# Cross-attention and routed FFN on one core: transposed activations stored by token tile in DRAM, and a store moved on ACT

## The reference

```python
a = einsum('bqd,bkd->bqk', layernorm(x), ctx)
x = x + einsum('bqk,bkd->bqd', softmax(a), ctx)
n = layernorm(x)
base = einsum('bsi,oi->bso', n, base_w) + base_b       # 2048 x 2048
h = einsum('bsi,ri->bsr', n, A)                        # rank 64
probs = softmax(einsum('bsi,ei->bse', n, router_w))    # 16 experts
topw, topi = top_k(probs, 2); topw /= sum(topw) + 1e-6
x = x + base + 0.5 * sum over the two experts of topw * (h @ B[expert].T)
```

## Time and profile before

| what | us |
|---|---|
| median of 3 runs | 1431.38 (1430.12 to 1438.4) |
| the profiled execution | 1436.82 |
| its span | 1433.4 |
| PE busy | 1361.7 (95%) |
| DVE busy | 935.2 (65%) |
| ACT busy | 623.8 (44%) |
| POOL busy | 320.4 (22%) |
| PE granted clock, mean | 0.989 |

### The profile page before, as it was taken

One profiled execution on the slowest core, in us unless ns is written; L12 is line 12 of the kernel. 1 busy time (PEld: TensorE's weight loads), 2 busy tenths in 40 slices (PEclk: granted clock), 3 DMA queues, 4 the chain that ended last, 5 costly groups with the idle time before them and its releaser, 6 DMA issues.

```text
span 1433.4 us, 18364 instructions
## 1 busy us (share of the span) xinstructions
PE 1361.7 (95%) x6777; PEld 1106.7 (77%) x6777; DVE 935.2 (65%) x1179; ACT 623.8 (44%) x777; POOL 320.4 (22%) x247
## 2 busy tenths in 40 slices
PE   5999999999999999999999999989989999999998
PEld 4778787787878778786888777767777888888886
DVE  5576777778677777768565476766767744644553
ACT  3355554535564554555421366765766400101000
POOL 2002002020201102020614733544444011111110
PEclk9999999999999999999999999999999999999999
DMA  8968678587867858669757697999995998788783
GB/s 287 293 204 271 197 249 257 199 250 246 267 202 249 262 194 249 229 226 239 206 163 185 181 301 216 297 315 280 290 299 119 337 269 257 242 245 255 241 242 125
DMA packets 206520, 345.34 MB, mean 241 GB/s; under 512 B 26912, under 2 KB 119072, under 8 KB 196768
## 3 DMA queue, kind: packets, MB, share of 16 engines
q1 hardware_dynamic: 187872, 277.06, 64.3%
q0 software_dynamic: 10528, 52.85, 12.1%
q10 hardware_dynamic: 8064, 14.68, 2.9%
HBM read 260.87 MB, written 99.41 MB: 251 GB/s over the span
## 4 chain that ended last, share of the span: by engine, by line
PE 35%; DMA 11%; DVE 3%; issue 2%; ACT 2%; POOL 1%; SPq 0%; ACTq 0%; POOLq 0%; DVEq 0%
PE scores L849 11%; PE scores L850 11%; PE scores L851 11%; DMA res<-x_scratch 5%; DMA y_scratch<-y_out,yrow_i 5%; PE work L885 1%; DMA w_in<-in_wT_dram 1%; PE work L886 1%; ACT b_hl L1069 1%; ACT y_out L1077 1%; DVE a_l L1419 1%; DVE raw_l L1176 1%; DMA hs_scratch<-hg,pos_i 0%; DVE w_l L1410 0%; DVE b_hl L1462 0%
## 5 line engine op out<-in xcount | busy, mean ns | idle before, releaser
L849 PE MATMUL scores<-w_h,a_h 128*128 128x512 f32 x896 | 353.4, 394 | 3.0 <-issue 3.0
L851 PE MATMUL scores<-w_h,a_l 128*128 128x512 f32 x896 | 351.9, 393 | 0.0
L850 PE MATMUL scores<-w_l,a_h 128*128 128x512 f32 x896 | 351.9, 393 | 0.0
L1053 ACT ACTIVATE a_h<-a_in 128x512 fp32r<-128x512 f32 x148 | 83.8, 622 | 320.5 <-DMA a_in<-xT_scratch 223.7
L849 PEld LDWEIGHTS scores<-w_h,a_h 128*128 128x128 f32 x896 | 169.6, 189 | 40.8 <-issue 3.4
L851 PEld LDWEIGHTS scores<-w_h,a_l 128*128 128x128 f32 x896 | 169.3, 189 | 38.1
L850 PEld LDWEIGHTS scores<-w_l,a_h 128*128 128x128 f32 x896 | 169.5, 189 | 37.2
L1176 DVE TENSOR_TENSOR raw_l<-raw_in,val_h 128x512 fp32r<-128x512 f32 x192 | 154.9, 827 | 43.8 <-ACT val_h L979 43.5
L715 PE MATMUL scores<-ctxT_h,nT_h 128*112 128x494 f32 (+1 forms) x512 | 174.8, 342 | 6.9 <-DVE x L1212 3.3
L1419 DVE TENSOR_TENSOR a_l<-a_in,a_h 128x512 fp32r<-128x512 f32 x148 | 110.5, 794 | 103.8 <-ACT a_h L1053 100.2
L717 PE MATMUL scores<-ctxT_h,nT_l 128*112 128x494 f32 (+1 forms) x512 | 171.6, 335 | 0.0
(11 more groups left out here) (149 smaller groups left out, 1979.2 us busy)
## 6 DMA issues: line engine op xcount, KB each, us to landing
ctxT_in<-in_ctxT_dram SPq DMA_DIRECT2D x64, 750.0 KB, 7.3
raw_in<-in_ctx_dram SPq DMA_DIRECT2D x32, 1280.0 KB
a_in<-xT_scratch SPq DMA_DIRECT2D x37, 1024.0 KB, 7.8
w_in<-in_wT_dram SPq DMA_DIRECT2D x32, 512.0 KB, 9.3
x<-in_x_dram SPq DMA_DIRECT2D x8, 1792.0 KB, 10.1
xT_scratch<-xT_st SPq DMA_DIRECT2D x8, 1792.0 KB, 11.8
res<-x_scratch SPq DMA_DIRECT2D x56, 256.0 KB, 7.4
y_add<-y_scratch SPq DMA_DIRECT2D x56, 256.0 KB, 5.6
```

Of the source, the lines that this page charges most:

```text
L849: pe.matmul(o, ah, wh, start=(k == 0), stop=False)
L850: pe.matmul(o, ah, wl, start=False, stop=False)
L851: last = pe.matmul(o, al, wh, start=False, stop=(k == KD - 1))
```

## The change

`xT_scratch` becomes [128, 14, 16, 128]: partition, token tile, block of D, token. A token tile is then 8 KB in one run per partition, and `load_a` reads it so. A batch of 224 tokens straddles tiles, so `store_xT` issues one DMA for each tile that it touches: two or three (128+96, 32+128+64, 64+128+32, 96+128 tokens, twice over), 20 in all. All waits on `xT_stored` count pieces. Because the pieces depend on the batch, the loops over the middle batches are unrolled on SP and on POOL; those of PE, ACT and DVE stay. On ACT, in visits 12 to 26, `store_tile(g - 1)` moves from before the visit's slot tiles to behind the first one's `rows_out` and `expert_high`.

```diff
-    xT_d = nc.dram_tensor("xT_scratch", [P, KD, T], F32).ap()
+    xT_d = nc.dram_tensor("xT_scratch", [P, TT, KD, P], F32).ap()
...
+        def pieces_of(b):
+
+            first, last = b * LQ, (b + 1) * LQ
+            return [(t, max(first - t * P, 0), min(last - t * P, P))
+                    for t in range(first // P, -(-last // P))]
+
+        def xT_count(batches):
+            return 16 * sum(len(pieces_of(b)) for b in range(batches))
...
             def store_xT(b):
                 sp.wait_ge(xT_staged, (b + 1) * NX)
-                sp.dma_start(xT_d[:, :, bass.ds(b * LQ, LQ)], xT_st[:, :, :]).then_inc(xT_stored, 16)
+                for t, lo, hi in pieces_of(b):
+                    sp.dma_start(xT_d[:, t, :, lo:hi], xT_st[:, :, t * P + lo - b * LQ:t * P + hi - b * LQ]
+                                 ).then_inc(xT_stored, 16)
...
             def load_a(v):
                 t = tile_of(v if v < PAIRED else PAIRED + 2 * (v - PAIRED))
-                sp.dma_start(a_in[A_SLOT[v]][:, :, :], xT_d[:, :, t * P:(t + 1) * P]).then_inc(a_loaded[A_SLOT[v]], 16)
+                sp.dma_start(a_in[A_SLOT[v]][:, :, :], xT_d[:, t, :, :]).then_inc(a_loaded[A_SLOT[v]], 16)
...
-            with sp.Fori(1, NB - 1) as b:
+            for b in range(1, NB - 1):
                 one(b, "mid")
...
                     if g > 1:
                         tile_high(g + 1, range(KD // AQ) if g in ROUTING else (0, 1))
-                    store_tile(g - 1)
+                    if g not in Y_TILES:
+                        store_tile(g - 1)
...
                     rows_out(s)
                     if s + 2 < SL:
                         expert_high(s + 2)
+                    if s == Y_TILES[g][0]:
+                        store_tile(g - 1)
...
             def stage_xT(stage, b, of):
-                if not (isinstance(of, int) and of == 0):
-                    at_least(pool, xT_stored, of * 16)
+                if of > 0:
+                    pool.wait_ge(xT_stored, xT_count(of))
...
-            with pool.Fori(1, NB - 1) as b:
+            for b in range(1, NB - 1):
```

More of the change, by code:

```diff
@@ L532, in one @@
                         load_w(j)
-                    sp.wait_ge(xT_stored, (NB - 2) * 16)
+                    sp.wait_ge(xT_stored, xT_count(NB - 2))
                     load_a(0)
@@ L647, in _ @@
             sp.wait_ge(val_used, NB * CH * NT)
-            sp.wait_ge(xT_stored, (NB - 1) * 16)
+            sp.wait_ge(xT_stored, xT_count(NB - 1))
             for g in range(GT):
@@ L666, in _ @@
                     sp.wait_ge(x2_stored, NB * 32)
-                    sp.wait_ge(xT_stored, NB * 16)
+                    sp.wait_ge(xT_stored, xT_count(NB))
                     sp.wait_ge(hn_stored, NB * 16)
@@ L1615, in entry_ids @@
             def entry_ids():
-                pool.wait_ge(xT_stored, NB * 16)
+                pool.wait_ge(xT_stored, xT_count(NB))
                 ids = count_i[:, 0:2 * TT].rearrange("p (i t) -> p i t", i=2)
```

## The result

| | kernel before | changed kernel |
|---|---|---|
| median of 9 runs each, side by side | 1437.35 us | 1424.88 us (1421.13 to 1429.64) |
| the profiled execution | 1436.82 | 1424.49 |
| its span | 1433.4 | 1422.7 |
| PE busy | 1361.7 | 1355.1 |
| PE granted clock, mean | 0.989 | 0.996 |

The ratio is 0.9922, with a 95% interval from 0.9901 to 0.9942. By this ratio the change takes away 11 us (8 to 14 by the interval), where the forecast said 18. The time lies inside the range, but outside the case I called likeliest (1401 to 1419): the direction held, and the size did not. The kernel before stands 6 us above the median of 1431.38 that the forecast started from, so it is the differences that can be compared: 18 off 1437.35 would have been 1419.

What follows compares the result with a forecast made beforehand. TensorE was held in 877.4 to 1088.0 us by scatters behind `res` loads made late by load_a's 512 B packets. Terms -20 - 1 + 1 + 2 = -18 off the median 1431.4 gave 1413 us, range 1400 to 1430 us.

Steps and rivals of the forecast that it cites:

- the case I called likeliest: Whole kernel: the summed gains and costs hold, 1401 to 1419 us, chance 0.60.
- the term for `load_a`: Expert visits 15 to 25: `load_a` in 8 KB runs, 2048 packets becoming 128, saves 20 us, between 16.3 and 29.1.
- What bounds the kernel: 877.4 to 1088.0 us, eleven visits: TensorE not full; at 16.5 us a visit, 29.1 us could be won.
- load_a, the lower bound (16.3 us): Expert stretch: tile packets at POOL's 8 KB price free 261 engine-us, 16.3 us over 16 engines, if the engines stay the limit.
- load_a, the value of 20: Expert stretch: `res` leaves SP at once, lands some 9 us after load_a; 20 us taken between the two ends.
- Add_bias then no longer holds the scatters: POOL in the expert stretch: with `res` early, add_bias stops holding the scatters for 12 to 15 us.
- The upper bound, 335 GB/s: Expert stretch at TensorE's pace: 60.77 MB in 181.5 us, below 406 GB/s of one microsecond, so all 29.1 us could go.
- The rival "the engines stay the limit": Expert stretch: `res` lands early but scatters wait for each other on engines about 99% busy; about 1426 us, chance 0.16.
- store_tile at no cost: ACT, visits 12 to 26: the moved part store goes out later but within some 2 us of slack, so 0.
- Store pieces: Middle batches: 20 pieces for 8 stores, a three-piece batch in 12 to 16 us, mostly hidden; cost +1, bounds 0 and 6.
- The hand-over (+2): Hand-over to the base matmuls: store pieces shift the queue, 0 to 4 us late; cost +2, bounds 0 and +9.
- Visits 9 to 11 (1 us): Visits 9 to 11: the `res` load frees POOL's row scatters a little sooner, a gain of 1 us.

Runs made afterwards that it cites:

- Layout and bytes together: Changed kernel (8 KB tile runs), with expert loads fetching 16 of 64 rows from slot tile 13 on, against the kernel before: 1408.37 us, ratio 0.9792.
- both orders: Changed kernel with SP's `res` load ahead of the a_in load and POOL's add_bias behind the scatters, against the kernel before: ratio 0.9898.
- add_bias behind: Changed kernel with POOL doing add_bias(g + 2) behind the scatters of visits 12 to 26, against the kernel before: ratio 0.9883.
- second trace of the changed kernel: The changed kernel run once more without an edit, against the kernel before: ratio 0.9905.

## Why the prediction was right in direction and wrong in size

The step that failed is the term for `load_a`. It was sized at 20 us, on the ground that `res` lands some 9 us after `load_a` and add_bias then no longer holds the scatters. In the stretch 11.4 us were won. `res` landed in some 15 us in most visits, and kernels in which add_bias holds no scatter back were only 1 to 6 us faster by the ratios, within the noise. What the visits wait for is the work of the DMA engines: with 11.8 MB less to fetch they go at 17.2 us each.

- **What bounds the kernel: right, its worth a little high.** All of the gain came in the stretch that the earlier trace rows named. Layout and bytes together won 25.2 us there. The 29.1 came from taking the shortest visit, 16.5 us, for the pace of all; most undisturbed ones take 16.9.
- **load_a, the lower bound (16.3 us): failed.** It priced the tile packets at POOL's 50.8 engine-us per MB. SP's queue went from 67.6 (1053 for 15.58 MB) to 55.0 per MB (858), and saved 195 engine-us, not 261: 12.2 us instead of 16.3. Two choices can have made it too large: one price of 37.6 ns for all of SP's packets, whatever their size, and POOL's price for SP's loads. And it took all the engine time that is set free for time won. By all queues 17.3 us were set free and 11.4 won, since the engines no longer stayed 99% busy. The bound that I called the lower was neither a bound nor met.
- **load_a, the value of 20: failed at the `res` step.** "`res` lands some 9 us after load_a" took an even share of bytes for SP's queue. It landed in 12.5 to 16.4 us in most visits, behind 1 MB of its own queue, and that queue got less than half: from 989 to 1004 us, with the tile and `res` of visit 21 under way, it moved 1.40 MB to POOL's 2.69, with 36.5% of the engines to 57.4%. The rule of the Trainium skill (DMA: Bandwidth & Descriptors, "Queues, rings and completion order"), turns packet by packet, gives the even share only while both queues have packets waiting; the direction of the trace agrees, the half does not. POOL's wait fell from 85.0 to 69.0 us, not below 40.
- **"Add_bias then no longer holds the scatters", as the cause: fell.** The wait was real, but it was not the limit. Without it (2.4 us) the kernel is hardly faster (0.9883 against 0.9905 to 0.9922), and with it at 85.6 us and fewer bytes it is 14 us faster. I had followed one visit's chain to `res` and taken the last name in it for the cause.
- **The upper bound, 335 GB/s: out of reach.** I set it against the 406 of one microsecond. No kernel here with all its bytes had a mean over 320 in the stretch (318 over 172 us at a share of 1.01 with both orders, 320 over 180 us at 1.00 with add_bias behind). At 318 the 60.77 MB take 191 us, not 181.5. Single visits of the changed kernel did reach 334 and 343 GB/s, over 17 and 18 us, but not the stretch.
- **The rival "the engines stay the limit": its mechanism is the nearest to what happened**, with every second visit still at 18 to 21 us and a share of 0.97. Its mark, such visits while POOL's wait is gone, shows in the kernels with add_bias behind (visits of up to 22.9 us). I gave it 0.16 against 0.60, although showed 0.99. That its 1426 us are so near the 1424.88 is luck: they are 5 us off 1431.4, and the measured gain is 11 off a median that stood 6 higher. It halved 16.3 to 8 where the stretch gave 11.4, and took +3 for stores that cost 0.7 at most. And it doesn't tell why the layout is worth as much where the engines have room.
- **store_tile at no cost: right**, and nearly at no gain. ACT waits for the scatters instead of `out_ready`.
- **Store pieces: direction right, the added time two to three times too high.** 8.9 us a three-piece batch, not 12 to 16; the 260 B row and the 32 ns of loads were both poor neighbours, and the read-modify-write below 512 B that the Trainium skill names (DMA: Bandwidth & Descriptors, "Specifications") shows in no number here. The holes took the rest, as argued.
- **The hand-over (+2): wrong term.** I left out that the `fresh` store, stuck behind `load_a(0)`, would leave SP sooner, by 10 us as measured. By the timeline that paid for the pieces: the x2 store came no later, and TensorE waits 0.15 us more.
- **Visits 9 to 11 (1 us)** can't be seen: up to visit 15 the sum of all is +0.7, and the same mark lies at 874.47 us in the second trace of the changed kernel, 3.6 earlier, so that sum is within the noise of single executions.

## What to carry to other kernels

Before following a chain of waits to a name, divide the bytes of the stretch by the time the bound engine would need (here 335 GB/s). If that is above every mean over a visit in the trace (here 312), suspect the DMA engines, and take a wait in the chain for the one that came last until a run without it says more. The surest test was to leave bytes out and see the stretch speed up with the suspected wait still there. Here moving bytes to a stretch with room gained 0.4 to 0.6%, reordering issues 0.1 to 0.4%, and neither is clear of the noise. What fewer packets are worth did not follow from the engine time they free: it was about the same where the engines had room. A row that prices a small packet holds for its neighbours and its direction only; a price from the same queue, direction and packet size is to be preferred to one from another.

## What was unexpected of the hardware

- Strided stores of 128 to 512 B packets went at 689 packets per us, and of 64 to 256 B at 959, where the 260 B runs into hs_scratch went at 386. In single microseconds of the changed kernel, 512 B packets went at 611 (247 to 248 us, 313 GB/s) and 256 B packets at 849 (250 to 251 us, 217 GB/s). Smaller packets cost less each, with no step below 512 B that made one dearer.
- A `res` load right behind a tile load of 2048 packets stayed in issue for 2 to 13.6 us in the expert visits, behind 128 packets of 8 KB with the same bytes for 0.43 to 1.23 us.
- Over 172 to 180 us the mean rate did not pass 320 GB/s at shares of 1.00 to 1.01, while single microseconds reach 406.
